# The last stage of a fused block: out projection and turns in the steps without an FFN down projection

## The reference

```python
x = u                                            # (2, 4096, 256)
a = layernorm(x)
z = rmsnorm(a, pre_w) @ in_proj.T                # 768 channels
z = causal_conv3(z) + short_b;  x2, x1, v = split(z)
xv = x1 * v
y = (long_conv(xv, h) + xv * D_skip) * x2        # h: 16 poles per channel, length 4096
y = y @ out_proj.T + a                           # the out projection
zm = rmsnorm(y, post_w)
mlp = (gelu_tanh(zm @ l1.T) * (zm @ l2.T)) @ l3.T    # 256 -> 672 -> 256, the MLP
x = x + layernorm(y + mlp)
# second half: an FFN 256 -> 1024 -> 256, whose two weights get rank-one
# updates made from 16 tokens of the sequence itself, one set for each sequence
n = layernorm(x)
h = gelu(n @ (W1 + scale*m1).T + b1)
x = x + layernorm(h @ (W2 + scale*m2).T + b2)
```

## Time and profile before

| | |
|---|---|
| median of 3 runs | 1172.92 us (1171.37 to 1175.77) |
| the profiled execution | 1170.21 us, span 1168.5 us |
| PE busy | 1068.5 us |
| DVE busy | 880.3 us |
| ACT busy | 721.5 us |
| mean granted clock of TensorE | 0.966 |
| stage C | from about 300 us to the end |

### The profile page before, as it was taken

How to read it: one execution, slowest core, us unless ns; L and a number is a source line. 1 busy time by engine, 2 the same in 40 slices (tenths; PEclk the granted TensorE clock), 3 DMA queues, 4 the chain that set the end, 5 groups by cost and what they waited for, 6 DMA issues and landing times.

```text
span 1168.5 us, 25495 instructions
## 1 busy us (share of the span) xinstructions
PE 1068.5 (91%) x9280; PEld 1031.2 (88%) x9280; DVE 880.3 (75%) x2311; ACT 721.5 (62%) x1609; POOL 285.2 (24%) x560
## 2 busy tenths in 40 slices
PE   3989999499388899999999999998999999999996
PEld 3989999367287899999999999988999999999996
DVE  5989998355158887778787777788787787887774
ACT  5867887366246566656665656665666656666643
POOL 5676664640000111111111111111111111111111
PEclk9989999699689899999999999998999999999999
DMA  3223221788564333333333333353233332333000
GB/s 118 82 82 109 77 87 56 229 243 248 79 141 62 44 50 64 47 55 47 50 55 68 49 55 46 66 136 48 46 53 66 53 55 46 49 54 65 26 20 28
DMA packets 109005, 89.23 MB, mean 76 GB/s; under 512 B 7072, under 2 KB 103616, under 8 KB 108752
## 3 DMA queue, kind: packets, MB, share of 16 engines
q1 hardware_dynamic: 107344, 85.16, 35.6%
q0 software_dynamic: 672, 2.39, 0.6%
q10 hardware_dynamic: 864, 0.05, 0.0%
HBM read 62.12 MB, written 17.07 MB: 68 GB/s over the span
## 4 chain that ended last, share of the span: by engine, by line
PE 51%; ACT 8%; issue 7%; DVE 5%; DMA 1%; SPq 1%; POOL 1%; ACTq 0%; DVEq 0%; POOLq 0%
PE ps_ring L1318 24%; PE ps_w L1318 13%; PE ps_m L1318 8%; PE ps_o L1318 3%; PE ps_rt L1328 2%; ACT gate L1008 2%; ACT frow L1015 2%; ACT pt_h L1002 2%; ACT ht_h L1027 1%; ACT hid L1030 1%; DVE base L1173 1%; DMA yin<-seq 1%; POOL sc L948 1%; PE ps_m L1364 1%; DVE bn L1083 1%
## 5 line engine op out<-in xcount | busy, mean ns | idle before, releaser
L948 POOL TENSOR_TENSOR sc<-sc,neg_half 128x2 f32<-128x2 f32 x128 | 95.5, 746 | 778.3 <-DVE sc L1273 485.8
L1008 ACT ACTIVATE gate<-ps_ring 128x256 f32<-128x256 f32 x192 | 72.8, 379 | 150.0 <-PE ps_ring L1318 149.2
L1318 PE MATMUL ps_ring<-mt_l,wl_h 128*128 128x256 f32 x640 | 130.5, 286 | 6.7 <-DVE mt_l L1095 6.7
L1318 PE MATMUL ps_ring<-mt_h,wl_h 128*128 128x256 f32 x640 | 130.5, 286 | 6.4 <-ACT mt_h L1072 6.4
L1318 PE MATMUL ps_ring<-mt_h,wl_l 128*128 128x256 f32 x640 | 129.7, 285 | 0.0
L1030 ACT ACTIVATE hid<-ps_ring,b1s 128x256 f32<-128x256 f32 x256 | 111.6, 483 | 17.0 <-DVE ht_l L1095 16.0
L1121 DVE TENSOR_TENSOR prod<-ps_ring,gate 128x256 f32<-128x256 f32 x192 | 80.9, 421 | 48.1 <-ACT gate L1008 46.1
L1318 PE MATMUL ps_ring<-xt_h,we_h 128*128 128x256 f32 x512 | 106.1, 288 | 8.4 <-ACT hid L1030 6.3
L1318 PEld LDWEIGHTS ps_ring<-mt_h,wl_h 128*128 128x128 f32 x640 | 101.4, 196 | 7.7 <-ACT mt_h L1072 4.4
L1318 PEld LDWEIGHTS ps_ring<-mt_l,wl_h 128*128 128x128 f32 x640 | 101.3, 195 | 7.5 <-DVE mt_l L1095 7.5
L1095 DVE TENSOR_TENSOR ht_l<-hid,ht_h 128x256 fp32r<-128x256 f32 x256 | 101.2, 423 | 6.3 <-ACT hid L1030 1.8
(11 more groups left out here) (170 smaller groups left out, 2761.9 us busy)
## 6 DMA issues: line engine op xcount, KB each, us to landing
toep<-taps_scratch SPq DMA_DIRECT2D x32, 512.0 KB, 4.7
xa<-in_x SPq DMA_DIRECT2D x16, 512.0 KB, 4.7
x_scratch<-x2c SPq DMA_DIRECT2D x16, 512.0 KB, 3.5
x2s<-x_scratch SPq DMA_DIRECT2D x32, 256.0 KB, 7.1
yin<-seq SPq DMA_DIRECT2D x128, 64.0 KB, 6.3
xa_c<-in_x SPq DMA_DIRECT2D x32, 256.0 KB, 2.7
xb_c<-in_x SPq DMA_DIRECT2D x32, 256.0 KB, 2.7
out<-frow SPq DMA_DIRECT2D x32, 256.0 KB, 5.8
```

What stands on the lines that cost most here:

```text
L948: nc.gpsimd.tensor_tensor(sc[:, to], sc[:, to], neg_half[:, 0, 0:CC], ALU.pow).then_inc(S[done], 1)
L1008: nc.scalar.activation(gate[rows_of, m % 2], ring[m % RING][rows_of, 0], ACT.Gelu_apprx_tanh).then_inc(S["gate_done"], 1)
L1318: mm = nc.tensor.matmul(out, lhs(a, kk), rhs(b, kk), start=(j == 0), stop=(closed and j == len(todo) - 1))
```

## The change

`early(n)` names the steps without an FFN down projection of their own: 0, 1, 2 and 18. `bare(n)` names 0 and 1, which have no unit h either.

- In steps 0 and 1 PE does `out_projection(n + 1)` behind block 3 of the MLP. In steps 2 and 18 it does it, and `turn_second(u)` behind it, ahead of `ffn_up`.
- In all four PE does `turn_scaled(n + 1)` between the two halves of `mlp_down(n)`.
- ACT squares and scales the rows behind the gates in steps 0 and 1 (into `frow` instead of `rows`, without the table loads), and between hidden blocks 1 and 2, and 4 and 5, in steps 2 and 18.
- DVE makes y (`gate_y`) two products sooner in steps 1, 2 and 18, and at the end of step -1 for n = 1. It adds the input and takes the mean of squares sooner, and makes `mt_l` ahead of the sum of y and MLP.

The other steps keep their order. SP's and POOL's programs are the same.

```diff
--- before.py
+++ after.py
@@ -871,6 +872,17 @@
         def late(w):
 
             return valid(w, UC) and w % UCB == 0
+
+        def early(n):
+
+            return valid(n, UC - 1) and (not valid(n - FFN_AT, UC) or late(n - FFN_AT))
+
+        def bare(n):
+
+            return valid(n, FFN_AT)
+
+        def scaled_in(n):
+            return frow if bare(n) else rows
 
         block = ctx.enter_context(nc.Block())
 
@@ -1015,20 +1027,37 @@
                     nc.scalar.activation(frow[:, c], frow[:, c], ACT.Identity, scale=sc[:, 2, c:c + 1],
                                          bias=shift[:, 2, c:c + 1]).then_inc(S["f_norm"], 1)
 
-            def hidden(h):
-                if h == 0:
+            def hidden(h, m):
+                if h == m == 0:
                     act.wait_ge(S["consts_in"], 16 * 3)
-                wait(act, S["w2_mm"], h)
-                for m in range(HB):
-                    b = HB * h + m
-                    act.wait_ge(S["h_mm"], b + 1)
-                    block_of = ring[(m + 2) % RING][:, 0]
-                    if m % 2 == 0:
-                        nc.scalar.activation(ht[0][:, m], block_of, ACT.Gelu, bias=b1s[:, m:m + 1]
-                                             ).then_inc(S["hh_even"], 1)
-                    wait(act, S["hl_done"], b - HIDS + 1)
-                    nc.scalar.activation(hid[:, m % HIDS], block_of, ACT.Gelu,
-                                         bias=b1s[:, m:m + 1]).then_inc(S["hid_done"], 1)
+                if m == 0:
+                    wait(act, S["w2_mm"], h)
+                b = HB * h + m
+                act.wait_ge(S["h_mm"], b + 1)
+                block_of = ring[(m + 2) % RING][:, 0]
+                if m % 2 == 0:
+                    nc.scalar.activation(ht[0][:, m], block_of, ACT.Gelu, bias=b1s[:, m:m + 1]
+                                         ).then_inc(S["hh_even"], 1)
+                wait(act, S["hl_done"], b - HIDS + 1)
+                nc.scalar.activation(hid[:, m % HIDS], block_of, ACT.Gelu,
+                                     bias=b1s[:, m:m + 1]).then_inc(S["hid_done"], 1)
+
+            def square_rows(n, made):
+                act.wait_ge(S["yrow_done"], n + 2)
+                wait(act, S["rms_arg"], n + 1)
+                if not bare(n):
+                    wait(act, S["xt_mm"], n)
+                    if made is not None:
+                        act.wait_ge(S["lora_out"], 16 * (made + 1))
+                for c in range(CC):
+                    nc.scalar.activation(scaled_in(n)[:, c], yrow[:, (n + 1) % 2, c], ACT.Square,
+                                         accum_out=sums[:, c:c + 1]).then_inc(S["squared"], 1)
+
+            def scale_rows(n):
+                act.wait_ge(S["rms_done"], n + 2)
+                for c in range(CC):
+                    nc.scalar.activation(scaled_in(n)[:, c], yrow[:, (n + 1) % 2, c], ACT.Copy,
+                                         scale=sc[:, 3, c:c + 1]).then_inc(S["zm_done"], 1)
 
             for n in steps():
                 u, h, w = n - 1, n - FFN_AT, n - OUT_AT
@@ -1044,9 +1073,18 @@
                             high_parts(first, (LORA // 2 + m,))
                         if m == 3 and valid(w, UC) and not late(w):
                             last_norm(w)
+                if n >= FFN_AT and valid(n, UC):
                     load_table(ACT.Gelu)
+                if bare(n):
+                    square_rows(n, made)
+                    scale_rows(n)
                 if valid(h, UC):
-                    hidden(h)
+                    for m in range(HB):
+                        hidden(h, m)
+                        if early(n) and m == 1:
+                            square_rows(n, made)
+                        if early(n) and m == 4:
+                            scale_rows(n)
                 if valid(w, UC) and (late(w) or not valid(n, UC)):
                     last_norm(w)
                 if valid(u, UC):
@@ -1054,19 +1092,11 @@
                     wait(act, S["h_mm"], HB * u)
                     nc.scalar.activation(xt[0][:], ps_t[:], ACT.Copy).then_inc(S["xh_done"], 1)
                 if valid(n + 1, UC):
-                    act.wait_ge(S["yrow_done"], n + 2)
-                    wait(act, S["rms_arg"], n + 1)
-                    wait(act, S["xt_mm"], n)
-                    if made is not None:
-                        act.wait_ge(S["lora_out"], 16 * (made + 1))
-                    for c in range(CC):
-                        nc.scalar.activation(rows[:, c], yrow[:, (n + 1) % 2, c], ACT.Square,
-                                             accum_out=sums[:, c:c + 1]).then_inc(S["squared"], 1)
-                    act.wait_ge(S["rms_done"], n + 2)
-                    for c in range(CC):
-                        nc.scalar.activation(rows[:, c], yrow[:, (n + 1) % 2, c], ACT.Copy,
-                                             scale=sc[:, 3, c:c + 1]).then_inc(S["zm_done"], 1)
-                    load_table(ACT.Gelu_apprx_tanh)
+                    if not early(n):
+                        square_rows(n, made)
+                        scale_rows(n)
+                    if not bare(n):
+                        load_table(ACT.Gelu_apprx_tanh)
                     act.wait_ge(S["zt_mm"], n + 2)
                     wait(act, S["ml_mm"], FB * (n + 1))
                     nc.scalar.activation(zt[0][:], ps_t[:], ACT.Copy).then_inc(S["zh_done"], 1)
@@ -1213,13 +1243,39 @@
                 nc.vector.tensor_tensor(frow[:], frow[:], x1[:, w % KEPT], ALU.add
                                         ).then_inc(S["out_done"], 1)
 
+            def gate_at(n, m):
+
+                part = m if early(n) else m - 2
+                if valid(n + 1, UC) and n > 0 and part in range(3):
+                    gate_y(n + 1, part)
+
+            def add_input(n):
+                dve.wait_ge(S["xhat_done"], CC * (n + 2))
+                dve.wait_ge(S["o_mm"], n + 2)
+                nc.vector.tensor_tensor(yrow[:, (n + 1) % 2], ps_o[:], xa[:], ALU.add
+                                        ).then_inc(S["yrow_done"], 1)
+
+            def mean_square(n):
+                dve.wait_ge(S["squared"], CC * (n + 2))
+                wait(dve, S["zm_done"], CC * (n + 1))
+                nc.vector.tensor_scalar(sc[:, 3], sums[:], 1.0 / D, EPS_RMS, ALU.mult, ALU.add
+                                        ).then_inc(S["rms_arg"], 1)
+
+            def scaled_low(n):
+                dve.wait_ge(S["zh_done"], n + 2)
+                split_low(zt[1][:], ps_t[:], zt[0][:], "zl_done")
+
             for n in steps():
                 u, h, w = n - 1, n - FFN_AT, n - OUT_AT
                 made, first = batch_of_rows(n), batch_of_weights(n)
+                if n == -1:
+                    for part in range(3):
+                        gate_y(0, part)
                 if valid(w, UC) and not late(w):
                     last_sum(w)
                 if valid(n, UC):
                     mlp_product(n, 0)
+                gate_at(n, 0)
                 if valid(w, UC) and not late(w):
                     last_variance(w)
                 if valid(u, UC):
@@ -1228,24 +1284,24 @@
                     low_part(first, 0, "weight_low1")
                 if valid(n, UC):
                     mlp_product(n, 1)
+                gate_at(n, 1)
                 if first is not None:
                     low_part(first, 1, "weight_low1")
                 if valid(n, UC):
                     mlp_product(n, 2)
                 if first is not None:
                     low_part(first, 2, "weight_low1")
-                if valid(n + 1, UC):
-                    gate_y(n + 1, 0)
+                gate_at(n, 2)
                 if valid(n, UC):
                     mlp_product(n, 3)
                 if first is not None:
                     low_part(first, 3, "weight_low1")
-                if valid(n + 1, UC):
-                    gate_y(n + 1, 1)
+                gate_at(n, 3)
+                if bare(n):
+                    add_input(n)
                 if valid(n, UC):
                     mlp_product(n, 4)
-                if valid(n + 1, UC):
-                    gate_y(n + 1, 2)
+                gate_at(n, 4)
                 if valid(n, UC):
                     mlp_product(n, 5)
                 if late(w):
@@ -1253,9 +1309,15 @@
                     last_variance(w)
                 elif valid(w, UC) and valid(n, UC):
                     output(w)
+                if bare(n):
+                    mean_square(n)
+                elif early(n):
+                    add_input(n)
                 if valid(h, UC):
                     for m in range(HB):
                         hidden_low(h, m)
+                        if early(n) and m == 2:
+                            mean_square(n)
                 if valid(w, UC) and (late(w) or not valid(n, UC)):
                     output(w)
                 if valid(u, UC):
@@ -1263,15 +1325,11 @@
```

(60 more changed lines are left out.)

## The result

The changed kernel takes 1182.17 us (median of 6 runs, 1179.39 to 1186.06) against 1172.68 of the kernel before (6 runs beside them, 1171.37 to 1175.77): ratio 1.0085, 95% interval [1.0066, 1.0103]. That is 0.9% slower; the prediction was 1183. The profiled execution took 1182.26 around a span of 1180.5 us, the one of before 1170.21 around 1168.5.

A forecast was written before the change was run, and what follows sets the result against it. TensorE, busy 91%, was taken as the bound, with VectorE's queue beside it at the edited steps. Order +2.3, clock 4.8 and 3.0, sum +10.1 us: profiled 1170.21 becomes 1180.3, median 2.7 above, 1183; range 1171 to 1191.

The forecast's parts named there:

- the order: Effect of the new order at full clock: +0.8 us over steps 0 to 3, +1.5 at 18 and 19, together +2.3.
- the clock: TensorE falls to 1.2 GHz behind new waits: 4.8 us in steps 3 and 19, 3.0 in 0, 1, 2, 18.
- step 0: MLP down projection ends at 338.4, 1.0 us late at full clock; slow matmuls 1.6 us at chance 0.8, so 1.3.
- step 1: Takes 20.75 us against 21.9 at full clock, gain 1.15; slow matmuls 3.0 us at chance 0.9, so 2.7.
- step 2: Takes 27.4 us against 25.5 at full clock, loss 1.9, with out projection and second turn ahead of FFN up projection.
- blocks of 3: At full clock step 3's block 5 ends 14.3 us after step 2's MLP down projection, before 15.25: gain 0.95.
- steps 18 and 19: Same walk as step 2: step 18 ends 2.3 us late, blocks behind it end after 14.3 against 15.1; +1.5.
- Step 3: TensorE waits 6.5 us after four blocks for product 0, due 11.8 us after step 2's end; slow clock behind, 2.4.
- Rival 1: Only the long waits, in steps 3 and 19, lower TensorE's clock: +7.1 us, 1180; chance 0.17.
- Rival 2: The clock costs no more than before, waits elsewhere swallowing slow matmuls: +2.3 us, 1175; chance 0.13.
- Rival 3: Faster: VectorE keeps up and the gaps at turns, 18.7 us, close: 1154, or 1164 with half; chance 0.10.
- The table loads: Steps 0 and 1 lose two ScalarE loads each, 1.28 us apiece; sum unchanged; possible 1.3 us return twice taken as nought.

The follow-up runs named there:

- a5: Changed kernel with unused matmuls in the new TensorE waits of steps 0, 1, 2, 3, 18 and 19; 1.0043 of the kernel before.
- a3: Changed kernel with 44 unused matmuls behind block 3 of steps 3 and 19; 1.0068 of the kernel before.
- a1: The change kept in steps 0 and 1 alone, steps 2 and 18 as before; 1.0040 of the kernel before.
- a4: Changed kernel with VectorE's last two low parts of the second FFN weight moved behind product 1 of steps 3 and 19; 1.0096 of the kernel before.
- c1: Kernel before with 20 unused matmuls ahead of the blocks of steps 1, 2, 3 and 19; 0.9963 of the kernel before.
- b1: The change in steps 0 and 1 alone, with y of n = 2 made in step 0; 0.9994 of the kernel before.
- d0: Kernel before with y of n = 1 and 2 made one step ahead and no table loads in steps 0 and 1; 0.9975 of the kernel before.
- d2: Kernel before with y of n=1 and 2 a step earlier, no table loads in steps 0/1, unused matmuls at start and heads of steps 1, 2, 3, 19; 0.9967.

## Why the prediction was right, step by step

The direction, the places of the waits and the sum held. The predicted loss was +10.1 us; 0.85% of 1172.68 is 10.0, and the medians differ by 9.5. Of the two terms of the sum, the order was put too small and the clock agrees with the runs within their width, so that the sum is right to 0.1 us is partly luck. Two readings of the kernel before were wrong: that its low clock in step 3 cost nothing, and that its clock stayed up behind M(1).

**The order** was put at +2.3. a5, whose clock is kept up where the change lets it fall (but for that one stretch in step 2), stands at 1.0043, +5.0 us [2.6, 7.6]; its trace gives +3.95 over the edited rows of the table. Step by step, predicted and then a5 less before: step 0 +1.0 and +1.28; step 1 -1.15 and -0.66; step 2 +1.9 and +2.02; blocks of 3 -0.95 and -1.30; steps 18 and 19 +1.5 and +2.6. Most of the miss is step 18: I carried over step 2's walk, M(18) +2.3, and a5 has +3.7. One profile says this roughly: step 18 takes 28.0 to 30.5 us, 29.1 in the mean, in the nine kernels that don't change it, and 31.7 to 32.8, 32.2 in the mean, in the five that do, so +3.1. VectorE in a5 shows an operation that the walk left out. The output of w, which step 2 does not have, stands ahead of the sum that the squares wait for, and hidden block 2 waits for the squares.

```profile
792.25 0.69 DVE L1243 TENSOR_TENSOR frow<-frow,x 128x512 f32<-128x512 f32 x1
792.86 0.68 DVE L1255 TENSOR_TENSOR yrow<-ps_o,xa_c 128x512 f32<-128x512 f32 x1
```

That this 0.69 us is a cause of the excess is argued; it was not tried by itself.

**The clock** was put at 7.8 (4.8 and 3.0). By the ratios of a5 and the change it is 4.9 us, from 1.6 to 8.2. By the table, after less a5, it is 8.1: step 0 2.8 (of which about 1.1 is the late rise of the next paragraph), step 1 1.6, step 2 0.7, the blocks of 3 and 19 1.7 and 1.6, step 18 -0.3. So the size of this term is not shown to be wrong, and not closely confirmed either.

Place by place: behind the waits of steps 3 and 19 the 18 matmuls of blocks 4 and 5 cost 1.70 us more (15.62 against 13.92 in a3), where 1.8 was predicted, and the first eight matmuls behind them took 1.25 and 1.69 us against 1.11 in step 19 of a5, so 0.1 and 0.6 more, where 0.6 was predicted. Step 0's down projection took 6.01 us from 331.92 to M(0) = 337.93, and in a5 4.44: 1.6 for a wait of 2.84 us, as predicted. Step 1 took 22.84 against 21.23: 1.6, where I had 2.7; but the same code takes 22.61, 22.61 and 23.88 in a1, a4 and a3, which makes 1.4 to 2.7. In steps 2 and 18 I had placed the falls ahead of the turn. They came behind the wait for y's low part, ahead of the up projection, and in step 18 nothing came of it (31.68 against 32.01); there, I argue, the waits behind took it back.

**Step 0** shows how little one profile tells. M(0) = 337.93 stands near the predicted 338.4 only because S was 3.55 us earlier in this execution: counted from S it came 4.1 us later, with 1.0 + 1.3 predicted. From the first block (317.09) to the second out projection (325.50) passed 8.41 us; in a3, whose program is the same up to there, 7.35. The clock was 1.00 from 323.0 in the one and from 320.7 in the other, with the same work before it, and about 1 us of the 4.1 is that.

**Step 3** went as forecast: TensorE waited 5.96 for product 0 (6.5 predicted), which came at M + 11.1 (11.8 predicted, 11.2 before), with the clock at 0.50 behind it.

**What was wrong in the step, not in its size:** "Before, the low stretch of step 3 stood beside VectorE's work and cost nothing." c1 took it away and won 1.4 us there and 1.3 in step 19. In step 3 this holds over all profiles: 14.8 to 15.7 us in the four with this order and nothing put in (before, a1, b1, d0), 13.8 in c1. In step 19 it hangs on the execution: a1 has 13.88 and d0 14.14, where the clock fell late and for a shorter stretch, before 15.09 and b1 15.79. The proof is in who waits. In c1 TensorE has four blocks done when product 0 comes, waits 0.65 us for it, and has 18 matmuls left:

```profile
389.62 0.50 PE L1318 MATMUL ps_ring<-mt_h,wl_h 128*128 128x256 f32 x2 [0.65 <-DVE prod L1121]
```

In the kernel before, product 0 came at the same point, 395.95 or M(2) + 11.17, but TensorE, slowed, ran on from there without a wait to 400.02, 4.1 us at 0.1175 us a matmul, some 34 of them: it was the bound itself by then. VectorE's 4.92 busy us of 5 were no proof of cover. The kernel before loses 4.3 us by its clock (0.37% [0.15, 0.58]), not the little I took it for. At equal clock the change costs far more than against the real kernel before: a5 over c1 is 1.0043/0.9963 = 1.0080, 9.4 us, and 8.4 by the table (to the blocks of 3 +5.2, steps 18 and 19 +3.2). The clock that the change loses replaces one already lost. The forecast's sum did not suffer by this error, as it started from the measured times of before, in which that loss is contained.

**The rivals.** Rival 1, only the long waits lower the clock, is refuted. A wait of 2.84 us was followed by clock 0.51, and so was the one of 3.24 by 0.50 (next two windows). The prediction's argument for this rival, that the clock stayed at 1.00 behind M(1) of the kernel before, misread: the window ends too soon. The clock fell 1 us behind its end, as the third window, the kernel before's, shows, though none of the waits there was longer than 1.4 us.

```profile
343.20:346.80 3.60, 0.39 (x4) 0.19 (x2) 3.60 (x11) 1.80 (x5) 0.50 (x1) 1.00 0.19 64
346.90:350.30 3.40, 3.40 (x16) 3.40 (x17) 1.04 (x3) 0.00 (x0) 0.00 (x0) 0.50 0.82 174
```

```profile
364.80:368.10 3.30, 3.30 (x17) 3.30 (x17) 2.75 (x12) 0.90 (x2) 0.69 (x1) 0.50 0.63 193
```

Rival 2, +2.3 and nothing for the clock, falls with a5: by the ratios 4.9 us, at least 1.6, come back when it is kept. Its heading, that the clock costs no more than before, is not refuted: by the ratios the change loses 4.9 us by its clock and the kernel before 4.3, and these two cannot be told apart. Rival 3, VectorE keeps up, was decided where it was said to be, at M + 5.66. Product 0 started at M(0) + 4.9 in step 1, in time, but at M(1) + 7.4 and M(2) + 11.1, and TensorE waited. It held in one place out of four.

**The table loads** did not come back: Square runs 0.02 us behind a gate made with the tanh table. (ScalarE's timeline.)

```profile
329.15 0.38 ACT L1020 ACTIVATE gate<-ps_ring 32x256 f32<-32x256 f32 x1
329.55 0.42 ACT L1053 ACTIVATE frow<-yrow 128x256 f32<-128x256 f32 x1
```

## What to carry to other kernels

Closing a gap at a hand-over moves the bound to the next queue. Find when the other engine has the operand ready (here VectorE's product 0, M + 5 to M + 11), and count how far the first engine can run ahead; the wait comes back there. Operands of a moved operation move with it: the reordering stopped losing in step 1 only when y was made a step sooner (b1), and making it too soon put a wait for a transfer ahead of the critical sum (d2). Where a wait cannot be removed, unused matmuls in it keep TensorE's clock up; that alone was worth 0.37% here (c1). They may even hold back the first real matmuls, as long as the next wait covers it: in c1 the blocks of step 3 began 3.8 us behind M(2) instead of 3.1, and the wait for mt_l behind them ended at M(2) + 5.5 in both.

## What the runs showed of the hardware

- The clock falls behind short waits. A single one of 2.84 us was enough in the changed kernel (0.51 in the window behind it), and one of 2.26 in a5. Interrupted ones were too: behind M(1) and M(2) of the kernel before, gaps of 4.45 and 5.0 us with 1.38 and 1.36 us of work in them, no single wait over 1.9 us, were both followed by 0.50. The Trainium skill ("TensorE: Matmul & The Clock Gate", Part 1, What's actually happening) speaks of idleness and sustained work; here idleness that was broken by short work lowered the clock as well.
- The fall can come after the wait, when the matmuls already run again: behind step 0's wait, which ended at 331.92, the clock was 1.00 to 333.2 and 0.50 after that. A window over the gap alone does not show it, and this is how was misread.
- The same program does not have its falls at the same places in every execution. In the blocks of step 19, unedited and with nothing put in, that made 13.88 to 15.79 us.
- TensorE's pace at clock 1.00 is not one number. In the kernel before, two matmuls of 256 columns mostly came every 0.2265 us from 400 to 560 us, and in much of the stretch from 560 to 900 every 0.236. The runs with the shortest row "to M(17)", a3 and b1 with 367, had the faster pace through nearly all of it, so this drift is a likely source of that row's spread; it was not tried by itself.
